# Attention with a relative position bias: maxima from pairs of 64-row products, written-out loops, and two of eight low parts on VectorE

## What is computed

```
logits[q, k] = (q . k) / sqrt(32) + row_bias[q, row(k)] + column_bias[q, column(k)]
row_bias[q, x]    = q . pos_emb_h[x - row(q) + 63]
column_bias[q, y] = q . pos_emb_w[y - column(q) + 63]
out[q] = softmax(logits[q, :]) @ v
```

## Time and profile before

| | |
|---|---|
| median of 3 runs | 9187.87 us (9184.39 to 9202.88) |
| the profiled execution | 9187.98 us, its span 9185.4 us |
| busy share of the span | PE 90%, DVE 77%, POOL 73%, ACT 63% |
| bias attention in the span | from about 62 us to about 3180 us |
| mean granted TensorE clock | 0.939 |

### The profile page before, as it was taken

The page is one execution under the profiler, slowest core; times in us unless marked ns, Lnnn a source line. Parts: engine busy times, 40 slices in busy tenths (PEclk is TensorE's granted clock), DMA queues, the critical chain, the costliest instruction groups (busy, mean ns, idle before and its releaser), DMA issues. The chain is left out here.

```text
span 9185.4 us, 139845 instructions
## 1 busy us (share of the span) xinstructions
PE 8246.9 (90%) x42040; PEld 6695.8 (73%) x42040; DVE 7029.1 (77%) x7887; ACT 5755.2 (63%) x14820; POOL 6726.0 (73%) x3596
## 2 busy tenths in 40 slices
PE   6999999999999767899999999967999989888798
PEld 4766767667676533788888888855786868888775
DVE  6776767767677666899999999976777746999734
ACT  4877878778787634777777777732565633445304
POOL 3876868678696725899999999950686825999605
PEclk9999999999999977899999999988999999988898
DMA  2111111111111245544444444453000010000000
GB/s 93 28 40 30 41 40 31 39 30 41 27 41 33 65 163 207 144 106 105 109 104 107 106 106 108 107 189 142 29 26 18 23 50 19 1 1 1 20 8 19
DMA packets 480129, 596.14 MB, mean 65 GB/s; under 512 B 273736, under 2 KB 294480, under 8 KB 471568
## 3 DMA queue, kind: packets, MB, share of 16 engines
q1 hardware_dynamic: 479504, 588.17, 22.4%
HBM read 349.14 MB, written 157.03 MB: 55 GB/s over the span
## 5 line engine op out<-in xcount | busy, mean ns | idle before, releaser
L817 POOL TENSOR_TENSOR l_probs_low<-l_probs,l_probs_high 128x512 fp32r<-128x512 f32 x1792 | 2384.9, 1359 | 787.2 <-ACT l_probs_high L787 770.4
L1542 POOL TENSOR_TENSOR m_c_h<-m_h,m_c 128x2048 f32<-128x2048 f32 x520 | 2341.8, 4561 | 51.1 <-DVE m_h L1529 50.9
L1529 DVE TENSOR_TENSOR_SCAN m_h<-m_decay,m_ps_x 128x1024 f32<-128x1024 f32 x1040 | 2273.2, 2263 | 95.8 <-issue 67.8
L1442 PE MATMUL m_ps_y<-m_c_h,m_ident 128*128 128x256 f32 x8320 | 1981.7, 381 | 2.1 <-POOL m_c_h L1542 2.1
L873 DVE TENSOR_REDUCE l_max_by_row<-l_ps_all 128x8 f32<-128x512 f32 x2048 | 1358.5, 686 | 522.7 <-PE l_ps_all L636 444.1
L1442 PEld LDWEIGHTS m_ps_y<-m_c_h,m_ident 128*128 128x128 f32 x8320 | 1513.5, 191 | 173.2 <-POOL m_c_h L1542 4.0
L785 ACT ACTIVATE l_probs<-l_ps_all 128x512 f32<-128x512 f32 x2048 | 1238.8, 605 | 454.8 <-PE l_ps_all L677 310.9
L787 ACT ACTIVATE l_probs_high<-l_ps_all 128x512 fp32r<-128x512 f32 x2048 | 1234.3, 603 | 0.0
L2095 POOL TENSOR_TENSOR l_probs_low<-l_probs,l_probs_high 128x512 fp32r<-128x512 f32 x512 | 660.4, 1296 | 584.1 <-ACT l_probs_high L2078 567.6
L2548 POOL TENSOR_TENSOR s_late<-s_late,s_products 128x1024 f32<-128x1024 f32 x352 | 858.0, 2477 | 307.0 <-ACT s_products L2530 306.9
L1466 ACT ACTIVATE m_b_diagonals<-m_steps,m_b_rows 128x32 fp32r<-128x32 f32 x4160 | 966.7, 306 | 3.0 <-DMA m_b_rows<-b_t 3.0
(11 more groups left out here) (382 smaller groups left out, 13819.1 us busy)
## 6 DMA issues: line engine op xcount, KB each, us to landing
m_delta_u<-du_t SPq DMA_DIRECT2D x1040, 128.0 KB, 3.8
m_c<-c_windows SPq DMA_DIRECT2D x130, 512.0 KB, 4.3
l_q_and_row_bias<-l_q_parts SPq DMA_DIRECT2D x64, 512.0 KB, 5.0
du_t<-m_delta_u_high SPq DMA_DIRECT2D x128, 256.0 KB, 3.0
du_t<-m_delta_u_low SPq DMA_DIRECT2D x128, 256.0 KB, 3.0
ys<-m_y SPq DMA_DIRECT2D x256, 126.0 KB, 5.0
m_direction<-ys SPq DMA_DIRECT2D x12, 2048.0 KB, 13.7
l_xn<-xn SPq DMA_DIRECT2D x8, 2048.0 KB, 8.0
```

What stands on the lines that cost most here:

```text
L817: pool.tensor_tensor(pl[:, slot, :], pt[:, slot, :], f(ph[:, slot, :]), ALU.subtract).then_inc(low_pool, 1)
L1442: ins = pe.matmul(y_ps[:, group % 2, 0:DIRS * SPAN].rearrange("p (d t) -> p d t", d=DIRS), ident[:, :], ch[:, group % CH, :, n, :], start= ...
L1529: dve.tensor_tensor_scan(h[:, u % H, :], decay[:, pair % 2, ct, k % 2, :, :].rearrange("p n t -> p (n t)"), x_ps[:, u % X, :], 0.0, ALU.mu ...
L1542: pool.tensor_tensor(ch[:, group % CH, 2 * pair % DIRS:2 * pair % DIRS + 2, :, :].rearrange("p d n t -> p d (n t)"), h[:, 2 * pair % H:2 * ...
```

## The change

**Maxima.** A unit becomes a pair. Both products of a pair use 64 rows of the array: rows 0 to 63 hold q and the column bias of columns 0 to 31, rows 64 to 127 hold q again and the column bias of columns 32 to 63. Each product covers 16 rows of keys by 32 columns, again 512 keys wide, and the two go to two banks. So a block has 16 pairs in place of 32 units, 32 reductions as before (now 16 values each), and one more 128x256 operation in `take_maxima`. A pair waits until both banks of the pair before are reduced. Ten pairs stand in tiles 0 to 17, six in tiles 20 to 30.

**Tables.** The products that make the two biases read q unsplit in fp32. Those of the row bias use 32 rows and 64 columns of the array, those of the column bias 32 by 32 (16 in a job), and two products with the identity, 512 wide, place q in each column job. ScalarE copies only half of q; the split of q on VectorE, the copies `copy_q` and the rounded tables are gone. The low part of k is made by a copy and a subtraction on VectorE.

**Places.** The q jobs of the next head move to tiles 22 to 29 of block 6. Three pairs of the second block stand in `start`. The low part of the row bias for a head's first block is copied by ScalarE's queue, the high part, after a semaphore of its own, by SyncE's.

**Loops.** TensorE's heads are all written out, and the blocks of ScalarE and GpSimd inside a head.

**Low parts.** VectorE makes slots 1 and 5 of eight, GpSimd the other six.

```diff
-    DVE_SLOT = 5
+    DVE_SLOTS = (1, 5)
-    EARLY, READY = 12, 19
-    LAST = slice(L - TW, L)
+    EARLY, READY, FILL = 6, 19, 3
+    ASIDE = 2 * TW
+    LAST = slice(L - ASIDE, L)
+    plan = [(t - 10, "q", t) for t in range(NTB)]
+    plan += [(1, "w", 0), (1, "h", 0), (2, "w", 1), (3, "k", 7), (3, "w", 2), (4, "h", 1), (4, "w", 3), (5, "k", 6), (5, "w", 4),
...
             def copy_rows(it, j):
                 row, slot = it * NTB + j, j % 2
-                sp.wait_ge(shifted, row + 2)
-                for g in range(GROUPS):
-                    for first, part in ((D, rh), (D + NEAR, rl)):
+                for first, part in ((0, rh), (NEAR, rl)):
+                    if part is rh:
+                        sp.wait_ge(high_made, row + 1)
+                    elif j:
+                        sp.wait_ge(shifted, row + 2)
+                    else:
+                        break
+                    for g in range(GROUPS):
                         sp.dma_start(f(ql[first:first + NEAR, slot, g, :]), f(part[g * NEAR:(g + 1) * NEAR, :])).then_inc(ql_in[slot], 16)
...
-                else:
+                elif kind == "h":
                     for k in range(8):
                         x = 8 * t + k
-                        if kind == "h":
-                            table, moving = eh, qc[:, x * SIDE:(x + 1) * SIDE]
-                        else:
-                            table, moving = ew, qc[:, :].rearrange("d (x y) -> d y x", y=SIDE)[:, x, :]
-                        ins = pe.matmul(o[0:SIDE, k * SIDE:(k + 1) * SIDE], table[:, SIDE - 1 - x:2 * SIDE - 1 - x], moving, start=True, stop=True)
+                        ins = pe.matmul(o[0:SIDE, k * SIDE:(k + 1) * SIDE], raw_eh[TWO, SIDE - 1 - x:2 * SIDE - 1 - x],
+                                        q_raw[TWO, x * SIDE:(x + 1) * SIDE], start=True, stop=True)
+                else:
+                    by_column = q_raw.rearrange("d (x y) -> d y x", y=SIDE)
+                    for k in range(8):
+                        y = 8 * t + k
+                        for rows, first, out in ((THREE, SIDE - 1 - y, D), (TWO, SIDE - 1 - y + HALF, 3 * D)):
+                            pe.matmul(o[out:out + HALF, k * SIDE:(k + 1) * SIDE], raw_ew[rows, first:first + HALF], by_column[rows, y, :],
+                                      start=True, stop=True)
+                    for rows, out in ((TWO, 0), (THREE, 2 * D)):
+                        ins = pe.matmul(o[out:out + D, :], ident[rows, rows], by_column[rows, 8 * t:8 * t + 8, :], start=True, stop=True)
...
-            def max_unit(row, j, u):
-
-                pe.wait_ge(max_taken, row * UNITS + (u + 1))
-                at, keys = slice(j * TW + u // KC * P, j * TW + (u // KC + 1) * P), slice(u % KC * TW, (u % KC + 1) * TW)
-                pe.matmul(ps[:, MAX0 + u % 2, :], qm[:, at], km[:, keys], start=True, stop=True).then_inc(max_filled, 1)
+            def both_halves(at, chunk):
+                rows = slice(chunk * ROWS_EACH, (chunk + 1) * ROWS_EACH)
+                low, high = (k.rearrange("p (x y) -> p x y", y=SIDE) for k in (km[0:SIDE, :], k2[SIDE:P, :]))
+                pe.matmul(ps[:, MAX0, :], qm[0:SIDE, at], low[:, rows, 0:HALF], start=True, stop=True)
+                pe.matmul(ps[:, MAX0 + 1, :], qm[SIDE:P, at], high[:, rows, HALF:SIDE], start=True, stop=True).then_inc(max_filled, 1)
+
+            def max_pair(row, j, p):
+
+                pe.wait_ge(max_taken, row * (2 * PAIRS) + (2 * p + 2))
+                both_halves(slice(j * TW + p // QT * P, j * TW + (p // QT + 1) * P), p % QT)
...
             def start(it, off):
-                made(it, off, number["k", 6] + 1)
...
+                made(it, off, number["k", 5] + 1)
+                for p in range(FILL):
+                    max_pair(row + 1, 1, p)
+                for i in range(2):
+                    score(it + off, 0, i)
...
-            with pe.Fori(0, ITS - 1) as it:
+            for it in range(ITS):
                 for j in range(NTB):
-                    attend(it, j, j == NTB - 1)
-            for j in range(NTB):
-                attend(ITS - 1, j, False)
+                    attend(it, j, max(0, j + 3 - NTB) if it + 1 < ITS else 0)
...
+            def copy_low_rows(it, off):
+
+                act.wait_ge(shifted, it * NTB + (off * NTB + 2))
+                for g in range(GROUPS):
+                    act.dma_start(f(ql[NEAR:D, 0, g, :]), f(rl[g * NEAR:(g + 1) * NEAR, :])).then_inc(ql_in[0], 16)
...
             def take_maxima(row):
-                dve.wait_ge(max_taken, row * UNITS + UNITS + 2)
+                dve.wait_ge(max_taken, row * (2 * PAIRS) + (2 * PAIRS + 2))
+                chain.link(dve.tensor_tensor(mx64[:, :, :], mx2[:, :, 0, :], mx2[:, :, 1, :], ALU.max))
...
-                if kind == "q":
-                    ins = dve.tensor_tensor(qc[SIDE:P, cols], bank[SIDE:P, :], f(qc[SIDE:P, cols]), ALU.subtract)
-                elif kind == "k":
-                    ins = dve.scalar_tensor_tensor(k2[0:D, cols], bank[0:D, :], SCALE, f(km[0:D, cols]), ALU.mult, ALU.subtract)
+                if kind == "k":
+                    chain.link(dve.tensor_copy(k2[TWO, cols], f(km[0:D, cols])))
+                    ins = dve.scalar_tensor_tensor(km[TWO, cols], bank[TWO, :], SCALE, f(k2[TWO, cols]), ALU.mult, ALU.subtract)
```

More of the change, by code:

```diff
@@ L439, in units, with dve_tiles_before @@
         return part
     def pool_tiles_before(i):
-        return sum(k % SLOTS != DVE_SLOT for k in range(i))
+        return sum(k % SLOTS not in DVE_SLOTS for k in range(i))
+    def dve_tiles_before(i):
+        return sum(k % SLOTS in DVE_SLOTS for k in range(i))
     with Mem(nc, stage) as m:
@@ L586, in _ @@
             pe.wait_ge(const, 64)
-            pe.wait_ge(parts_ok, 1)
             pe.wait_ge(tables_ok, 1)
@@ L707, in attend @@
                 for i in range(KT):
-                    for block_of, u in units(j, i):
-                        max_unit(it * NTB + block_of, block_of, u)
+                    for block_of, p in pairs(j, i):
+                        max_pair(it * NTB + block_of, block_of, p)
                     if j + 1 < NTB:
@@ L933, in _ @@
                     row = it * NTB + j
-                    work = [(i + 1.6, take_low, row, i) for i in range(DVE_SLOT, KT, SLOTS)]
+                    work = [(i + 1.6, take_low, row, i) for i in range(KT) if i % SLOTS in DVE_SLOTS]
                     if row:
@@ L937, in _ @@
                     for i in range(KT):
-                        work += [(i + 0.8 + 0.05 * k, reduce_unit, it * NTB + block_of, u) for k, (block_of, u) in enumerate(units(j, i))]
+                        work += [(i + 0.8 + 0.05 * k + half / 100, reduce_half, it * NTB + block_of, p, half)
+                                 for k, (block_of, p) in enumerate(pairs(j, i)) for half in range(HALVES)]
                     if j + 1 < NTB:
```

216 lines of the change are left out of this document (102 added, 114 removed).

## The result

The changed kernel takes 9763.61 us (median of 4 runs, 9759.61 to 9766.34), the kernel before beside it 9195.38. The ratio is 1.0617, with a 95% interval of 1.0598 to 1.0635. The forecast was 9438, its range 9040 to 9510. So the sign and the likeliest case were right, and the forecast was less than half of what came: +250 forecast, +568 measured.

What follows compares the result with a forecast made beforehand. PE was taken to bound the kernel. Ordinary blocks 124, block 0 21, blocks 6 and 7 121, loops -36 and first preparation 20 sum to +250 on 9187.98, giving 9438 us, range 9040 to 9510.

Steps and rivals of the forecast that it cites:

- the likeliest case: Pairs at about 0.62 us, kernel near 9438, own range 9370 to 9520; chance 0.50.
- The pair: Two 64-row products on PE would cost 0.62 us, against 0.46 for two units.
- the three parts I gave: Of a pair's 0.62 us: 0.30 emptying the array twice and an unhidden load, 0.11 one load, 0.21 both products.
- both rivals: Pairs without a price: 0.23 us each, 9089, chance 0.35; division has no effect on fp32r: 0.46, 9275, chance 0.15.
- Ordinary blocks: Blocks 1 to 5 of each head: 44.3 us where it was 41.18, +3.1, times 40 is +124.
- the wait at tile 19: PE's wait before the turn in ordinary blocks, for VectorE's maximum: 1.5 to 2.7 us, taken as 1.8.
- Block 0: First block, eight times: 19 pairs for 44 units and a wait 1.0 longer, +2.6 us each, +21 in all.
- Blocks 6 and 7: Block 6 +9.5, block 7 +11, less 3.2 behind it: +17.3 us, seven times, +121 in all.
- I allow 4 of waiting where there were 16: Block 7 on PE: 4 us of waiting added to 89.4 of work, giving 93.4, +11.
- The transition: Behind block 7, PE's wait for the row-bias copies: 3.2 us less from fewer issues and an earlier high part.
- First preparation: First head's preparation: more table work against q copies and splits that go, +20 us (0 to 40).
- Loops: PE's "issue" wait at the loop's back edge goes: -6.0 us, six times, -36; ScalarE and GpSimd 0.

Runs made afterwards that it cites:

- a_same_rows: Changed kernel with both products of every pair on rows 0 to 63 of the array; 10010.39 us, ratio 1.0902.
- a_all_rows: Changed kernel with both products of every pair on all 128 rows and contiguous keys; 9521.61 us, ratio 1.0356.
- b_two_low: Kernel before with low-part slots 1 and 5 on VectorE in place of slot 5 alone; 9317.46 us, ratio 1.0144.
- a_turn_at_21: Changed kernel with the turn and the shift of ordinary blocks two tiles later, at tile 21; 9606.62 us, ratio 1.0456.
- b_best: Kernel before with TensorE's heads written out, turn and shift one tile later, and the changed kernel's row-bias copies; 9152.48 us, ratio 0.9957.
- b_loops: Kernel before with TensorE's heads written out in place of the loop, nothing else changed; 9156.07 us, ratio 0.997.

## Why the prediction was right in sign and wrong in size

**The pair.** 0.62 forecast, 0.63 measured. My reasoning from the earlier trace rows held, and so did the concurrency of the earlier trace rows, now for fp32r; the three parts I gave (0.30, 0.11, 0.21) are 0.40 and 0.23. By a_same_rows and a_all_rows both rivals are refuted: the visit has a price, and the products do run at once. The Trainium skill, TensorEngine Tiling (Array Packing), section Key Properties, has a change of tiling mode drain TensorE; the runs agree, with 0.40 us for the way in and out. The Trainium skill, TensorE: Matmul & The Clock Gate, Part 3 (Packing small matmuls), has products in different row groups start some 4 ns apart. Here too they do (3 or 4 ns in all 1024 pairs), but the gain of 0.23 is less than the 0.40 of the visit.

**Ordinary blocks.** Forecast 44.3, without a fall of the clock 45.2, on the mean 46.54: +214 us in place of +124. The step that failed is the wait at tile 19, taken at 1.8: it is 2.73. I priced the added 128x256 operation by L879, which reads a bank. L891 reads none and is held up by GpSimd's running operation: 1.48 in place of 0.42. That is 0.9 x 40 = 38. The other 1.3 x 40 = 52 are a term that my sum did not have: products at the lower clock behind that wait. b_two_low shows it without pairs, a_turn_at_21 shows pairs without it.

**Block 0**: +2.6 forecast, +2.7 measured.

**Blocks 6 and 7.** This is the largest miss. Forecast +17.3 with -6.0 for the loop in six of seven, measured +40.0 with the loop's gain inside it (seven times, +280 in place of +85). The step that failed is "I allow 4 of waiting where there were 16". The 16 were the time left over by my sum of work, and by the earlier trace rows they were not waiting: PE is busy for 75.42 of the 83.00 and stands for 7.6; the clock there is 0.93. So the sum struck out 12 us where PE stood for less, and with them, without a reason, what the lower clock costs. In the changed kernel the waits are 10.9: the pairs wait 8.1 for the reductions of both banks, PE 1.4 and 0.6 for the split of k, and 0.8 for two others. And the clock falls further. Taken from the two traces, on the mean of seven heads:

| blocks 6 and 7, us a head | before | after |
|---|---|---|
| time | 133.7 | 173.8 |
| PE stands | 17.4 | 14.0 |
| PE busy at the lower level | 11.9 | 55.3 |
| PE busy at full clock | 104.4 | 104.4 |

A product at the lower level costs about twice what it costs at full clock (0.43 and 0.23), so about half of the third row is the price of the clock: 6 and 28, an estimate. The head then lost 22 by the clock, which my sum had at nothing, and 22 by more work (the fourth row and the other half of the third), and won 3 of standing, where my sum had -12, -3.2 and the loop's -5. The work I had put too high, at +32 (9.5 and 22.7), and this hid 10 of the miss. Of its parts, the row job was forecast at 1.18 and measured at 1.07. The column job, forecast 3.1 and measured 3.14, came right by luck: its identity products are 1.81 and not 1.29, its 32 small passes 1.33 and not 1.76. The transition was to give 3.2; from the turn to the first score it takes 10.27 where it took 9.4, since three pairs now stand there and wait for each other (1.4 each); in the kernel before, the copies alone won 0.6 (b_best).

**First preparation**: +20 forecast, +46 measured (170.3 against 124.0). Counted in the same way, work is 12 of it, the clock 27 and standing 7; the sum had some 20 of work and nothing for the other two.

**Loops**: -36 forecast, b_loops gives -30, -36 between the profiled executions. The loop's "issue" wait behind block 7 is gone, as forecast.

Together: ordinary blocks +214, block 0 +19, blocks 6 and 7 +280, preparation +46, the last two blocks -2, and 14 behind the bias attention, in the part that varies anyway: 572 between the two profiled executions, to rounding. The range was too narrow because it held the waits' bounds but never the clock, which makes a wait of 2.7 us cost 4.2 in a block that is lengthened once.

## What to carry to other kernels

Ask what a visit to a smaller size of the array costs before halving the rows for two products at once: here each visit costs 0.40 us and wins 0.23. By these two figures two pairs in one visit would win 0.06, an estimate; no run here has it. Don't call the gap between a sum of work and a measured stretch waiting: read how long the engine stands, and at what clock it works. Price a wait of TensorE that grows past what the trace has with the clock behind it, and look at the granted clock of every window in which small products stand. Before moving a wait, look at what the other engine's queue holds behind the instruction that waits: an order with the shift behind one reduction won 0.6 us a block that moving the turn alone had not.
